# Message-passing layer: both parts of the edge means stacked on 128 partitions, 8 products of 128 rows a step for 12 of 64

## The chip, the core and the metric

The kernel runs on one core of a Trainium2 chip. A core has TensorE (PE, matrix products out of SBUF into PSUM; PEld is its weight load), VectorE (DVE), ScalarE (ACT), GpSimd (POOL), SyncE (SP, which here issues transfers) and 16 DMA engines. They run side by side and wait for one another by semaphores. The metric is the device time of one execution in microseconds, as a median of several runs.

## What is computed

6250 nodes with 256 features, 100,000 edges with 64 features. The edge features are averaged over the edges of each source node, joined with the node's features and a global vector, sent through two dense layers, added to the node's features and normalized:

```python
sums = jax.ops.segment_sum(edge_attr, src, num_segments=n)
counts = jax.ops.segment_sum(jnp.ones((edge_attr.shape[0],), edge_attr.dtype), src, num_segments=n)
edge_attr_agg = sums / jnp.maximum(counts, 1.0)[:, None]
u_expanded = u[batch]
combined = jnp.concatenate([x, edge_attr_agg, u_expanded], axis=1)
h = jax.nn.relu(combined @ W1 + b1)
return h @ W2 + b2
# and around it
x = _layernorm(x + that)
```

W1 has 448 rows (256 for x, 64 for the edge means, 128 for the global vector) and 512 columns, W2 is 512 x 256. All is float32.

## The kernel before

The program has three stages. In the **first** (to about 500 us) the edges are sorted by node in batches, and beside this the part of the hidden layer that depends on x and the global vector is computed into `pre`. In the **second** (about 500 to 735 us) the sorted rows are loaded in pairs of blocks (`sup`, issued by SP, 8 pairs a turn), DVE and ACT make `onehot` masks from them, and PE adds up the sums and counts of all nodes in its PSUM banks (L840). Between the first and the second turn of these loads SP also loads the 64 rows of W1 for the edge means (`w1e_raw`, L453) and W2 (L454). POOL, which has nothing else to do then, cuts both into a high part (as float32r, a shorter format) and a low part, the remainder (L545, L548).

The **third** stage, the layers, is the one that the change is in. DVE makes `means` (125 nodes on the partitions; 50 columns of nodes with 64 features) from the banks in eight instructions (L1166). Then 25 steps follow, each with two columns of 125 nodes, and two sets of buffers b = 0, 1 used in turn. A product in full precision is made of three of shorter ones: high by high, low by high, high by low. Step g consists of:

- `transpose_means` (PE, L864): the 125x64 means of each column, transposed to 64x125, into PSUM (`aggt_p`).
- `save_aggt` (ACT, L655): their high part, to SBUF (`aggt_high`, 64 partitions, 250 columns).
- `low_means` (DVE, L1181): PSUM minus the high part gives the low part (`aggt_low`).
- `first_layer_edges` (PE, L876): for each of 4 blocks of 128 hidden units three products of 64 rows by 250 columns, 12 in all, into `h_p`.
- `hidden_sum` (DVE, L1174): `h_p` added to `pre`, two instructions.
- `relu` (ACT, L661 and L666): `h_high`, the high part, in one instruction, then `pre` itself in two halves.
- `low_hidden` (POOL, L565): `h_low`, two instructions. After it POOL adds b2 to two columns of x (`add_b2`, L556, on `xs`), three steps ahead.
- `second_layer` (PE, L892): 24 products into `y_p`, of which 8 take `h_low`.
- `moments` (DVE, L1189 to L1198): z = y + xs, its statistics, mean and variance. z needs the store of step g-2 from the same buffer to have landed.
- `deviation` (ACT, L670), `finish_norm` (DVE, L1202 reciprocal, L1204 `shift`), `normalize` (ACT, L676), then the store (SP, L469).

Each engine takes its instructions in the order in which they are written, and this order is staggered over the steps. PE: transposes of g+2, L876 of g+1, L892 of g. DVE: moments of g, hidden_sum of g+2, low_means of g+3, finish_norm of g. ACT: deviation of g, save_aggt of g+3, relu of g+2, normalize of g. POOL: low_hidden of g, add_b2 of g+3. DVE and ACT run the first 20 steps as two rounds of a loop over 10 and write the last 5 out.

The lines that the change rewrites most:

```python
for w_part, part in ((0, 0), (1, 0), (0, 1)):
    last = nc.tensor.matmul(h_p[b][:, at:at + NW], w1er[w_part][:, k * P:(k + 1) * P],
                            aggt[b][part][:, :], start=(w_part == part == 0), stop=(part == 1))
```

## Time and profile before

| | |
|---|---|
| median of 3 runs | 879.79 us (876.77 to 879.95) |
| profiled execution | 875.59 us |
| its span in the trace | 873.6 us |
| its granted TensorE clock, mean | 0.972 |
| PE busy | 789.4 us, 90% |
| DVE busy | 702.8 us, 80% |
| ACT busy | 491.8 us, 56% |
| POOL busy | 438.8 us, 50% |
| the layers, from the first instruction on means | 736.70 us to the end |

The profile shows one execution. Its span is 2 us shorter than that execution's own time, and that time is 4.2 us under the median. A row of the timeline is an instruction (or a merged run of them) with its start, its length, its engine and line, and in brackets how long its engine had been idle before it and who ended that. Lengths of neighbours on one engine overlap a little. What an engine does while another holds up the end costs nothing, so shares of busy time are only the beginning.

### The profile page before, as it was taken

The numbers are of one execution on the slowest core, as the hardware profiler recorded it, in microseconds if no ns is written. First come the engines' busy times: TensorE is split into PE (matmuls) and PEld (weight loads), VectorE is DVE, ScalarE is ACT, GpSimd is POOL, SyncE is SP. The second block draws the span as 40 slices with busy tenths as digits, with TensorE's granted clock in tenths as the row PEclk, the third lists the DMA queues.
The fourth block names the chain that finished last, engine by engine and source line by source line (L and its number), as shares of the span: only waits on it lengthen the run. The fifth ranks groups of instructions, "written<-read, shape, count | busy, mean of one in ns | idle before, by whom it ended". The sixth has DMA issues, their size and how long they took to land.

```text
span 873.6 us, 32606 instructions
## 1 busy us (share of the span) xinstructions
PE 789.4 (90%) x11466; PEld 732.5 (84%) x11467; DVE 702.8 (80%) x2328; ACT 491.8 (56%) x998; POOL 438.8 (50%) x429
## 2 busy tenths in 40 slices
PE   5578999999999999999999679898988887999996
PEld 4367888989888999889999579898888886999995
DVE  8599978988888888888996078888889887577785
ACT  1143666556665666556666445555555553678775
POOL 3055667877777777777777220000001000678883
PEclk9778999999999999999999989999999999899998
DMA  8244677677667776677664289999997780011111
GB/s 196 89 135 138 185 165 230 202 222 230 209 205 215 230 231 207 210 221 229 198 191 168 92 292 271 288 278 277 281 277 231 221 250 27 18 55 49 59 59 61
DMA packets 170992, 161.40 MB, mean 185 GB/s; under 512 B 111654, under 2 KB 151705, under 8 KB 170830
## 3 DMA queue, kind: packets, MB, share of 16 engines
q1 hardware_dynamic: 152398, 102.18, 42.5%
q0 software_dynamic: 18560, 58.82, 19.2%
q8 instruction: 16, 0.26, 0.1%
q14 instruction: 18, 0.15, 0.1%
HBM read 95.32 MB, written 65.63 MB: 184 GB/s over the span
## 4 chain that ended last, share of the span: by engine, by line
PE 67%; DVE 9%; DMA 8%; POOL 6%; issue 6%; ACT 2%; SPq 1%; DVEq 0%; ACTq 0%; POOLq 0%
PE ps L840 22%; PE ps L785 20%; PE ps L892 8%; PE ps L717 7%; POOL sorted_rows L530 5%; PE ps L876 5%; DMA sorted_rows<-payload,idx 4%; DVE onehot L1135 2%; DVE perm L1045 2%; POOL sorted_rows L536 2%; DMA attr_buf<-in_edge_attr 1%; DMA where_d<-where 1%; ACT payload L586 1%; PE ps L734 1%; PE ps L772 1%
## 5 line engine op out<-in xcount | busy, mean ns | idle before, releaser
L530 POOL DMA_INDIRECT sorted_rows<-payload,idx x264 | 296.2, 1122 | 141.9 <-issue 56.4
L785 PE MATMUL ps<-attr_buf,perm 128*128 128x198 bf16 x3168 | 312.3, 256 | 16.9 <-DVE perm L1045 13.0
L785 PEld LDWEIGHTS ps<-attr_buf,perm 128*128 128x128 bf16 x3168 | 290.8, 97 | 35.0 <-issue 17.6
L586 ACT CAST payload<-ps 128x792 bf16<-128x792 f32 x264 | 213.3, 828 | 187.7 <-PE ps L785 164.1
L1045 DVE TENSOR_SCALAR perm<-place_of,pos 128x470 bf16<-128x470 int16 x792 | 234.6, 356 | 19.5 <-PE ps L785 18.0
L1135 DVE TENSOR_SCALAR onehot<-node_of,sup 128x256 bf16<-128x256 int16 x903 | 194.4, 286 | 60.1 <-PE ps L840 28.0
L840 PE MATMUL ps<-sup,onehot 128*128 128x65 bf16 x6192 | 202.2, 194 | 32.0 <-DVE onehot L1135 25.2
L840 PEld LDWEIGHTS ps<-sup,onehot 128*128 128x128 bf16 x6192 | 199.7, 98 | 34.7 <-issue 34.7
L642 ACT ACTIVATE apart<-node_of,sup 128x256 bf16<-128x256 int16 x129 | 65.5, 508 | 109.1 <-PE ps L840 104.3
L565 POOL TENSOR_TENSOR h_low<-pre,h_high 128x500 fp32r<-128x500 f32 x50 | 62.2, 1261 | 113.8 <-ACT pre L666 113.8
L717 PE MATMUL ps<-xt,w1x 128*128 128x125 f32 x800 | 100.0, 279 | 4.7 <-ACT xt L591 4.7
L556 POOL TENSOR_TENSOR xs<-xs,b_all 125x256 f32<-125x256 f32 x50 | 35.6, 733 | 134.9 <-DMA xs<-in_x 134.9
L717 PEld LDWEIGHTS ps<-xt,w1x 128*128 128x128 f32 x800 | 94.5, 194 | 6.6 <-ACT xt L591 5.8
L950 DVE TENSOR_TENSOR attr_buf<-attr_buf 128x576 f32<-128x576 f32 x88 | 66.0, 751 | 19.8 <-DMA attr_buf<-in_edge_attr 19.4
L597 ACT ACTIVATE pre<-ps,hid_bias 128x125 f32 (+1 forms) x200 | 56.7, 374 | 21.6 <-PE ps L717 21.6
L957 DVE TENSOR_TENSOR attr_buf<-attr_buf 128x576 f32<-128x576 f32 x88 | 65.4, 744 | 0.0
L645 ACT ACTIVATE onehot<-apart 128x256 bf16<-128x256 bf16 x129 | 53.8, 417 | 4.1
L892 PE MATMUL ps<-w_high,h_high 128*125 128x256 f32 x200 | 52.7, 296 | 0.0
L892 PE MATMUL ps<-w_low,h_high 128*125 128x256 f32 x200 | 50.0, 283 | 0.0
L661 ACT ACTIVATE h_high<-pre 128x1000 fp32r (+1 forms) x25 | 26.0, 1041 | 25.9 <-DVE pre L1174 25.9
L892 PEld LDWEIGHTS ps<-w_high,h_high 128*125 128x125 f32 x200 | 37.5, 188 | 3.3 <-issue 0.2
L963 DVE TENSOR_REDUCE pos<-ps 128x450 f32 (+1 forms) x44 | 27.4, 622 | 14.7 <-PE ps L772 13.8
(144 smaller groups left out, 686.5 us busy)
## 6 DMA issues: line engine op xcount, KB each, us to landing
sup<-sorted_rows SPq DMA_DIRECT2D x129, 396.0 KB, 4.1
attr_buf<-in_edge_attr SPq DMA_DIRECT2D x43, 576.0 KB
xs<-in_x SPq DMA_DIRECT2D x10, 560.0 KB
out<-z SPq DMA_DIRECT2D x25, 224.0 KB
x_stage<-in_x SPq DMA_DIRECT2D x47, 112.0 KB
sorted_rows<-payload,idx POOLq DMA_INDIRECT x264
pre<-jump_d SPq DMA_DIRECT2D x1, 1560.0 KB, 10.6
pre<-first_d SPq DMA_DIRECT2D x1, 780.0 KB, 7.3
```

Of the source, the lines that this page charges most:

```text
L530: pool.indirect_dma_start(out=sorted_rows, out_offset=bass.IndirectOffsetOnAxis(ap=idx[:, n:n + 1], axis=0), in_=payload[s][:, :], in_offs ...
L565: nc.gpsimd.tensor_tensor(h_r[b][1][:, at:end], pre[:, g * KH * NW + at:g * KH * NW + end], h_r[b][0][:, at:end].bitcast(F32), ALU.subtrac ...
L586: nc.scalar.copy(payload[s][:, :].rearrange("p (r w) -> p r w", w=PART), slots_p[s % PSUM_BUFS]).then_inc(s_pay, 1)
L642: nc.scalar.activation(apart[k // 2 % 2][:, :], node_of[:, :], ACT.Abs, scale=-1.0, bias=place_in[k][:, ACT_SLOT, :]).then_inc(s_apart, 1)
L717: last = nc.tensor.matmul(pre_p[:, k * NP:(k + 1) * NP], w1x[:, c, k * P:(k + 1) * P], xt[:, c, :], start=(c == 0), stop=(c == KX - 1))
L785: last = nc.tensor.matmul(slot_p[s % PSUM_BUFS][r].rearrange("p (h f) -> p h f", f=PLANE), places, parts[:, :, s * BT + t, :, 1], start=(t ...
L840: last = nc.tensor.matmul(ps[:, bass.ds(at[k] + h * 512, ROW)], onehot[k % HOT_BUFS][:, r, h * P:(h + 1) * P], sup[k][:, r, part * PLANE:p ...
L892: last = nc.tensor.matmul(y_p[b][0:NP, c * DIM:(c + 1) * DIM], h_r[b][part][:, at:at + NP], w2r[w_part][:, k * DIM:(k + 1) * DIM], start=( ...
L950: nc.vector.tensor_tensor(attr_buf[a][:, 1, at, 0:FEAT], attr_buf[a][:, 0, at, 0:FEAT], high, ALU.subtract).then_inc(s_rest, 1)
L957: nc.vector.tensor_tensor(attr_buf[a][:, 2, at, 0:FEAT], attr_buf[a][:, 1, at, 0:FEAT], middle, ALU.subtract).then_inc(s_low, 1)
L1045: last = nc.vector.tensor_scalar(perm[s][:, t, :], place_of[:, :], pos[:, bass.ds(c * CT + (s * BT + t), 1)], None, ALU.is_equal)
L1135: last = nc.vector.tensor_scalar(onehot[k % HOT_BUFS][:, r, :], node_of[:, :], place_in[k][:, r, :], None, ALU.is_equal)
```

## The change

W1's 64 rows for the means are loaded twice, one above the other, on 128 partitions, and the high part is made of both copies. The low part has its 64 rows above 64 rows of zeros. DVE splits the means before they are transposed: a copy gives the high part, a subtraction the low part, both into `mean_parts`, 64 features beside 64. One transpose of 125x128 then brings the high part on partitions 0 to 63 and the low part on 64 to 127, and ACT saves all 128 with one copy (`aggt`). The first product of a block is W1's doubled high part by both parts (two of the three products before), the second is the low part above zeros by the same (the third). So each step has 8 products of 128 rows for 12 of 64.

`low_means` goes; `split_means` comes, two instructions on DVE, and stands ahead of `moments` in a step. `transpose_means` waits for it. Four of the eight means instructions come before the first two splits, four after.

```diff
-        w1er = [sb(f"w1e_{part}", [FEAT, HID], F32R) for part in ("high", "low")]
-        w1e_raw = sb("w1e_raw", [FEAT, HID])[:, :]
+        w1er = [sb(f"w1e_{part}", [P, HID], F32R) for part in ("high", "low")]
+        w1e_raw = sb("w1e_raw", [P, HID])[:, :]
...
-        aggt = [[sb(f"aggt{b}_{part}", [FEAT, NW], F32R) for part in ("high", "low")] for b in range(2)]
+        mean_parts = [sb(f"mean_parts{b}", [P, 2, 2, FEAT], F32R) for b in range(2)]
+        aggt = [sb(f"aggt{b}", [P, NW], F32R) for b in range(2)]
...
-            sp.dma_start(w1e_raw, w1[DIM:DIM + FEAT, :]).then_inc(s_w2, 16)
+            for half in range(2):
+                sp.dma_start(w1e_raw[half * FEAT:(half + 1) * FEAT, :], w1[DIM:DIM + FEAT, :]).then_inc(s_w2, 16)
...
-            for n, (low, whole, high) in enumerate(((w1er[1], w1e_raw, w1er[0]), (w2r[1], w2_raw, w2r[0]))):
-                pool.wait_ge(s_w_hi, n + 1)
-                nc.gpsimd.tensor_tensor(low[:, :], whole, high[:, :].bitcast(F32), ALU.subtract).then_inc(s_w_lo, 1)
+            nc.gpsimd.memset(w1er[1][:, :].bitcast(F32), 0.0).then_inc(s_w_hi, 1)
+            for n, (low, whole, high) in enumerate(((w1er[1][0:FEAT, :], w1e_raw[0:FEAT, :], w1er[0][0:FEAT, :]),
+                                                    (w2r[1][:, :], w2_raw, w2r[0][:, :]))):
+                pool.wait_ge(s_w_hi, 3)
+                nc.gpsimd.tensor_tensor(low, whole, high.bitcast(F32), ALU.subtract).then_inc(s_w_lo, 1)
...
             def transpose_means(g, b):
-                pe.wait_ge(s_aggt_lo, g + 1)
+                if g >= 2:
+                    pe.wait_ge(s_aggt, g - 1)
+                pe.wait_ge(s_mean_lo, g + 1)
                 for c in range(2):
-                    at = (g * 2 + c) * FEAT
-                    last = nc.tensor.transpose(aggt_p[b][:, c * NP:(c + 1) * NP], means[0:NP, at:at + FEAT],
-                                               ident[0:NP, 0:NP])
+                    both = mean_parts[b][0:NP, c, :, :].rearrange("p s f -> p (s f)")
+                    last = nc.tensor.transpose(aggt_p[b][:, c * NP:(c + 1) * NP], both.bitcast(F32), ident[0:NP, 0:NP])
...
             def first_layer_edges(g, b):
-                pe.wait_ge(s_aggt_lo, g + 3)
+                pe.wait_ge(s_aggt, g + 1)
...
-                    for w_part, part in ((0, 0), (1, 0), (0, 1)):
-                        last = nc.tensor.matmul(h_p[b][:, at:at + NW], w1er[w_part][:, k * P:(k + 1) * P],
-                                                aggt[b][part][:, :], start=(w_part == part == 0), stop=(part == 1))
+                    nc.tensor.matmul(h_p[b][:, at:at + NW], w1er[0][:, k * P:(k + 1) * P], aggt[b][:, :],
+                                     start=True, stop=False)
+                    last = nc.tensor.matmul(h_p[b][:, at:at + NW], w1er[1][:, k * P:(k + 1) * P], aggt[b][:, :],
+                                            start=False, stop=True)
...
-            def low_means(g, b):
-                dve.wait_ge(s_aggt, g + 1)
-                nc.vector.tensor_tensor(aggt[b][1][:, :], aggt_p[b], aggt[b][0][:, :].bitcast(F32),
-                                        ALU.subtract).then_inc(s_aggt_lo, 1)
+            def split_means(g, b):
+                dve.wait_ge(s_aggt_p, g + (PAIR - 1))
+                two = means[0:NP, bass.ds(g * (2 * FEAT), 2 * FEAT)].rearrange("p (c f) -> p c f", f=FEAT)
+                high, low = mean_parts[b][0:NP, :, 0, :], mean_parts[b][0:NP, :, 1, :]
+                nc.vector.tensor_copy(high, two).then_inc(s_mean_hi, 1)
+                dve.wait_ge(s_mean_hi, g + 1)
+                nc.vector.tensor_tensor(low, two, high.bitcast(F32), ALU.subtract).then_inc(s_mean_lo, 1)
...
             def step(m, s, left=STEPS):
                 g = m * PAIR + s
+                if left > 3:
+                    split_means(g + 3, 1 - s % 2)
                 moments(g, s % 2, m * PAIR + s // 2 * 2)
                 if left > 2:
                     hidden_sum(g + 2, s % 2)
-                if left > 3:
-                    low_means(g + 3, 1 - s % 2)
                 finish_norm(g, s % 2)
...
-            low_means(0, 0)
-            low_means(1, 1)
+            for k in (6, 7, 0, 1):
+                mean(k)
+            dve.wait_ge(s_agg, 4)
+            split_means(0, 0)
+            split_means(1, 1)
+            for k in (2, 3, 4, 5):
+                mean(k)
+            split_means(2, 0)
             hidden_sum(0, 0)
             hidden_sum(1, 1)
-            low_means(2, 0)
```

The places on which most depends. First DVE, in the loop over the steps, from the last instruction of hidden_sum on, as it was (line, operation, output and inputs, shape; ISA and REGISTER_ALU rows only compute addresses and waits):

```order
L1174 ISA
L1174 TENSOR_TENSOR pre<-ps,pre 128x2x2x125
L1180 REGISTER_ALU
L1181 TENSOR_TENSOR aggt1_low<-ps,aggt1_high 64x250
L1201 REGISTER_ALU
L1202 RECIPROCAL rstd<-std 125x2
L1204 SCALAR_TENSOR_TENSOR shift<-mv,rstd 125x2
L1185 ISA
L1189 ISA
L1189 TENSOR_TENSOR z<-ps,xs 125x256
```

Here the low part of the means stands between hidden_sum and the reciprocal, and z follows shift. The same place on DVE with the change:

```order
L1184 TENSOR_TENSOR pre<-ps,pre 128x2x2x125
L1214 REGISTER_ALU
L1215 RECIPROCAL rstd<-std 125x2
L1217 SCALAR_TENSOR_TENSOR shift<-mv,rstd 125x2
L1190 REGISTER_ALU
L1193 ISA
L1193 COPY mean_parts0<-means 125x2x64
L1195 TENSOR_TENSOR mean_parts0<-means,mean_parts0 125x2x64
L1198 ISA
L1202 ISA
L1202 TENSOR_TENSOR z<-ps,xs 125x256
```

The instruction behind hidden_sum is gone, and a copy and a subtraction stand between shift and the next z.

Second PE, at the start of the layers, from the end of the second stage on, as it was (`aggt0_high` is the high part of buffer 0):

```order
L850 MATMUL ps<-zeros 128x455 x6
L850 MATMUL ps<-zeros 128x260 x2
L864 MATMUL ps<-ident,means 64x125 x4
L876 MATMUL ps<-aggt0_high,w1e_high 128x250
L876 MATMUL ps<-aggt0_high,w1e_low 128x250
L876 MATMUL ps<-aggt0_low,w1e_high 128x250
```

Four transposes of means are followed by three products for each block. The same place with the change:

```order
L858 MATMUL ps<-zeros 128x455 x6
L858 MATMUL ps<-zeros 128x260 x2
L874 MATMUL ps<-ident,mean_parts0 128x125 x2
L874 MATMUL ps<-ident,mean_parts1 128x125 x2
L884 MATMUL ps<-aggt0,w1e_high 128x250
L886 MATMUL ps<-aggt0,w1e_low 128x250
```

The transposes now give 128 rows, and of each three products two are left.

## Rows read from the trace of the kernel before

**Rows 1.** Busy time by stretch: PE, PEld, DVE, ACT, POOL, clock, DMA share, GB/s.
```profile
690.00:700.00 10.00, 8.42 (x267) 8.30 (x264) 8.02 (x39) 5.05 (x12) 0.00 (x0) 1.00 0.75 216
740.00:750.00 10.00, 8.99 (x40) 8.18 (x41) 4.13 (x9) 3.52 (x6) 2.78 (x3) 0.52 0.00 0
770.00:780.00 10.00, 10.00 (x82) 9.35 (x81) 7.57 (x22) 7.76 (x15) 8.12 (x9) 1.00 0.16 51
```

**Rows 2.** Chain that ended last: start, length, what; a step, then the end.
```profile
795.06 1.59 PE ps L876 x12
796.65 3.02 PE ps L892 x24
799.67 0.22 PE ps L864 x2
...
857.69 0.77 DVE z L1189 x2
...
863.21 0.99 ACT z L676 x2
...
866.63 0.77 DVE z L1189 x2
```

**Rows 3.** Timeline of DVE at the start of the layers: start, length, idle before.
```profile
736.70 3.94 DVE L1166 TENSOR_TENSOR means<-ps,rcount 128x256 f32<-128x256 f32 x8
...
743.97 1.26 DVE L1174 TENSOR_TENSOR pre<-ps,pre 128x500 f32<-128x500 f32 x2 [2.69 <-PE ps L876]
...
751.66 0.75 DVE L1189 TENSOR_TENSOR z<-ps,xs 125x256 f32<-125x256 f32 x2 [2.71 <-PE ps L892]
```

**Rows 4.** Timeline of DVE in the layers, some instructions of several steps.
```profile
775.74 0.75 DVE L1189 TENSOR_TENSOR z<-ps,xs 125x256 f32<-125x256 f32 x2 [0.48 <-PE ps L892]
...
779.37 0.16 DVE L1204 SCALAR_TENSOR_TENSOR shift<-mv,rstd 125x2 f32<-125x2 f32 x1
...
784.31 0.61 DVE L1204 SCALAR_TENSOR_TENSOR shift<-mv,rstd 125x2 f32<-125x2 f32 x1
785.40 0.75 DVE L1189 TENSOR_TENSOR z<-ps,xs 125x256 f32<-125x256 f32 x2 [0.47 <-PE ps L892]
...
808.45 0.46 DVE L1204 SCALAR_TENSOR_TENSOR shift<-mv,rstd 125x2 f32<-125x2 f32 x1
```

**Rows 5.** Timeline of ACT: normalize, of the step whose z began at 775.74.
```profile
781.36 1.08 ACT L676 ACTIVATE z<-z,shift,rstd 125x256 f32<-125x256 f32 x2
```

**Rows 6.** Timeline of POOL in the layers.
```profile
781.01 2.49 POOL L565 TENSOR_TENSOR h_low<-pre,h_high 128x500 fp32r<-128x500 f32 x2 [0.84 <-ACT pre L666]
783.47 1.43 POOL L556 TENSOR_TENSOR xs<-xs,b_all 125x256 f32<-125x256 f32 x2
...
808.15 1.43 POOL L556 TENSOR_TENSOR xs<-xs,b_all 125x256 f32<-125x256 f32 x2
```

**Rows 7.** z alone (ns min/median/max) and shift in the groups (busy, mean ns).
```profile
L1189 DVE TENSOR_TENSOR z<-ps,xs x50: 411/419/426, 751.7 to 867.0; 125x256 f32<-125x256 f32 x50
...
L1204 DVE SCALAR_TENSOR_TENSOR shift<-mv,rstd 125x2 f32<-125x2 f32 x25 | 9.4, 377 | 0.9
```

**Rows 8.** The page, costliest groups: onehot's (busy us, mean ns, idle before).
```profile
L1135 DVE TENSOR_SCALAR onehot<-node_of,sup 128x256 bf16<-128x256 int16 x903 | 194.4, 286 | 60.1 <-PE ps L840 28.0
```

**Rows 9.** Timeline in the second stage: SP's queue, POOL and DVE.
```profile
504.60 0.63 SPq L453 DMA_DIRECT2D w1e_raw<-in_L_gnn_W  x1
...
517.31 2.34 POOL L548 TENSOR_TENSOR w_low<-z,w_high 128x1024 fp32r<-128x1024 f32 x1
...
517.39 2.35 DVE L1135 TENSOR_SCALAR onehot<-node_of,sup 128x256 bf16<-128x256 int16 x1 [2.81 <-PE ps L840]
```

**Rows 10.** Timeline of PE: second and last product of one step's L876.
```profile
800.04 0.27 PE L876 MATMUL ps<-aggt_high,w1e_low 64*128 64x250 f32 x1
...
801.20 0.28 PE L876 MATMUL ps<-aggt_low,w1e_high 64*128 64x250 f32 x1
```

**Rows 11.** Timeline of PE's weight loads: a pair of transposes of x.
```profile
307.79 0.23 PEld L708 LDWEIGHTS ps<-ident,x_stage 125*128 125x128 f32 x2
```

More of the change, by code:

```diff
@@ L267, in build @@
         y_p = [bank(4 + b) for b in range(2)]
-        aggt_p = [bank(6 + b, NW)[0:FEAT, :] for b in range(2)]
+        aggt_p = [bank(6 + b, NW) for b in range(2)]
         s_fill = sem("s_fill")
@@ L327, in build @@
         s_aggt = sem("s_aggt")
-        s_aggt_lo = sem("s_aggt_lo")
+        s_mean_hi = sem("s_mean_hi")
+        s_mean_lo = sem("s_mean_lo")
         s_h_p = sem("s_h_p")
@@ L654, in save_aggt @@
                 act.wait_ge(s_h_p, g + 1)
-                nc.scalar.copy(aggt[b][0][:, :], aggt_p[b]).then_inc(s_aggt, 1)
+                nc.scalar.copy(aggt[b][:, :], aggt_p[b]).then_inc(s_aggt, 1)
             def relu(g, b):
@@ L1144, in _ @@
             dve.sem_inc(s_z, 4)
-            dve.sem_inc(s_aggt_lo, 2)
             for b in range(2):
@@ L1163, in _, with mean @@
             mean_of = means[:, :].rearrange("p (b h f) -> p h b f", h=2, f=FEAT)
-            for k in (6, 7, 0, 1, 2, 3, 4, 5):
+            def mean(k):
                 lo, hi, sums = table_bank(k)
```

2 lines of the change are left out of this document (1 added, 1 removed).

## The prediction

> **What bounds the kernel now.** By the table above, TensorE (PE) is busy for 90% of the span at a granted clock of 0.972. The change touches only the last stage, the two layers over 25 steps, so next I read the busy time by stretch [rows 1]: there PE is busy all the time at clock 1.00, with VectorE (DVE) at 7.57 of 10 us, ScalarE (ACT) at 7.76 and GpSimd (POOL) at 8.12. All are loaded; PE is merely first. The chain of waits [rows 2] says the same: one step is 0.22 us of transposes, 1.59 us for the 12 products of L876 and 3.02 us for the 24 of L892, 4.83 us in all, and nothing else. It runs so from the first z at 751.66 us [rows 3] to that of step 22 at 857.69 us [rows 2]; this is 106.03 us for 22 steps.
>
> Then I followed the other engines through a step [rows 4 to 6], because a PE that gets faster is worth only what they leave. Write z(g) for the start of z in step g. It is 775.74 in one step and 785.40 two steps on, so 9.66 us for two; DVE is idle for 0.48 and 0.47 us before these. From z(g) a chain runs on: hidden_sum, ACT's h_high and pre, then POOL's two h_low instructions at 781.01, 5.27 us after z(g), then at once POOL's two xs additions from 783.47 us, ending at 784.90 us, 9.16 us after z(g). That last event is half a microsecond ahead of z(g+2). It matters if something on DVE has to wait for it.
>
> **Something does.** The shift instruction (L1204) works on 125x2 numbers, yet its mean is 377 ns [rows 7]. Asked for at 779.37 us it takes 0.16 us; asked for at 784.31 it lasts to 784.92 [rows 4], and POOL's second addition ends at 784.90. Asked at 808.45 it ends at 808.91, where the first of the two additions from 808.15 (1.43 us for both) ends, so it can slip in between two POOL instructions. Both inputs of shift are in SBUF. z has one of its two in PSUM, and its 50 instructions take 411 to 426 ns, whatever POOL is doing. An instruction with one tensor as its input shows the same in the stage before: a onehot, 286 ns on average on the page [rows 8], takes 2.35 us at 517.39 and ends just behind POOL's w_low (517.31, 2.34 us) [rows 9]. So some DVE instructions with all operands in SBUF stand still for as long as a POOL instruction runs. Today only shift does so in the layers, inside DVE's idle time.
>
> The Trainium skill, SBUF — State Buffer, section Who interferes with whom, gives this as a rule: a DVE instruction in a two-port mode (copies and scalar operations between SBUF tiles can be), or with two SBUF inputs while GpSimd reads SBUF, blocks fully against a GpSimd instruction. The rows above agree. It speaks against this change, because the old low_means read PSUM and one SBUF tile, and both instructions of the new split have only SBUF operands. Without it the sum would be that of the first rival.
>
> **Part 1, PE.** Eight products for twelve. Inside L876 ten starts take 1.16 us (800.04 to 801.20 [rows 10]), 0.116 us a product; these have 64 rows and 250 columns. Those of L892 have 128 rows and 256 columns and come at 3.02/24 = 0.126 us with their gaps, so 128 rows cost no more than 64 beyond the extra columns. Four fewer are -0.46 us a step. The transposes grow from 64 to 128 columns of means; their nearest row, the transposes of x (125x128, L708), has 0.23 us for the weight loads of a pair [rows 11], against 0.22 us for a pair here [rows 2], so I take 0. PE could then run a step in 4.37 us.
>
> **Part 2, DVE.** low_means (0.40 us) goes; split_means comes, ahead of moments: a copy of 125x128, a wait for it, a subtraction of 125x128. In the rows, 125x2 takes 0.16 us and 125x256 takes 419 ns [rows 4, 7], so 125x128 is half way, 0.29 us; the copy lies between the same ends, and I take 0.25 us. With a wait between and one on each side (I take 0.18 us for the three, more than the idle 0.01 to 0.1 us between instructions that follow without one) the pair is 0.72 us; bounds 0.42 (two at 0.16 and 0.1) to 1.14 (two at 0.419 and 0.3). Queued behind it are moments, hidden_sum and everything down to the output; and PE's transposes of that step, which used to be long free to go, now wait for its end.
>
> Where does it fit? DVE arrives at shift when POOL is at its additions. Then shift, copy and subtraction must come behind them: shift ends 9.18 us after z(g) (784.92), and 0.72 us more put z(g+2) 9.90 us after z(g) instead of 9.66. If the copy slips in between the two additions, POOL is put back by as much, which gives the same. The same holds for odd and even steps, since each POOL round starts from its own z. So **the step is 4.95 us, bound by DVE behind POOL, and PE idles 0.5 us of it**: +0.24 us for each of 11 pairs, +2.6 us. With the bounds of the split the pair of steps is 9.60 to 10.32 us, so -0.7 to +7.3 us. If only the subtraction waits and the copy runs beside POOL, the pair is shorter by the copy and its wait, about 9.6 us, -0.7 us in all: this counts as the same case.
>
> **Part 3, ACT.** save_aggt copies 128 rows instead of 64 in the same columns: as many columns as before, so as long, and ACT is busy for 7.76 of 10 us [rows 1]. Nothing.
>
> **Part 4, the start of the layers.** Before, the means (3.94 us) come first, then the two low parts and the first products, and hidden_sum at 743.97 us [rows 3]. Now four of the eight means instructions (about 1.9 us) and two splits (0.72 each, POOL idle here) come first; products start near 740.3 us, at a clock of about 0.52 [rows 1], the lower of its two levels (1.2 GHz, not 2.4), 8 at twice 0.116 us, 1.9 us, so h_p is ready at 742.2. DVE meanwhile does the other four means and a third split, to 742.8 us. hidden_sum is 1.2 us earlier. PE's next turn of L876 has four slow products less too, but L892 then waits a little for h_high and h_low. I take z(0) **1.5 us** earlier (0.8 to 2.2).
>
> **Part 5, the stage before.** SP issues a second load of the W1 rows between two turns of sup loads (0.63 us [rows 9]), 128 KB more through the DMA engines (216 GB/s at three quarters busy [rows 1]: 0.6 us at that rate, less if they have room); POOL's work on the weights, which blocks DVE, gets a memset of 128x512 (at most half of w_low's 2.34 us, which is on 128x1024). Bounds 0.2 to 1.8 us; **+0.8 us** taken: the loads are a turn ahead, which covers a part, but DVE's time is spent.
>
> **Part 6, the end.** From z(22) to the end, 15.9 us, nothing is removed: z(24) waits for the store of step 22 in the same buffer [rows 2].
>
> Sum: +2.6 - 1.5 + 0.8 = +1.9 us. The profiled execution took 875.59 us (span 873.6); 877.5 us for it, and on the median of 879.79 us, which lies 4.2 us above, 881.7 us.
>
> **Rivals.** (a) **DVE does not wait for POOL**: the split runs earlier in the step, in the time that shift stands still now. For it: the evidence is small operands and another stage; no row has this subtraction. Even then PE's 4.37 us isn't reached: from z(775.74) to the end of normalize (781.36 + 1.08) are 6.70 us, and in the tail normalize's end at 864.20 to z at 866.63 is 2.43 us, through the store that frees the buffer. That makes 9.13 us for two steps: 11 x -0.53 = -5.8, with the rest -6.5 us, 873.3 us. (b) **PE's saving is paid whole**: 24 steps x -0.46 = -11.0, with +0.8: 869.6 us. This needs the store to land 0.4 us sooner; nothing speaks for it. (c) **Slower**: the subtraction is asked for after POOL's next h_low has begun, and stands behind 1.25 us (half of 2.49 [rows 6]). The additions end 9.16 us after the z of two steps ago, h_low begins 5.27 us after the last z. After a short step of 4.58 us (PE's 4.37 and 0.2 to z) the additions end at 4.58, and the subtraction is asked for at about 4.98, 0.29 us ahead of h_low. It decides once the waits and the copy are 0.3 us longer than I take them. Price 1.25 us each; in 4 of 11 pairs 5.0 us: 886.7 us; in all, 14 us. (d) **The clock falls** in PE's new gaps: in the stage before PE was 84% busy at clock 1.00 [rows 1], so hardly; its price would be tens of microseconds.
>
> **How the numbers follow.** Half a per cent, 4.4 us, is about what a measurement here can tell from no change. The forecast has 0.56 (of that 0.04 beyond +4.4 us through its upper bound), (a) 0.20, (b) 0.04, (c) 0.18, (d) 0.02. Faster 0.24, same 0.52, slower 0.24. The forecast's own range is 877 (-0.7 - 2.2 + 0.2) to 888 us (+7.3 - 0.8 + 1.8); for 8 in 10 the range takes in (a) and a good part of (c): 873.0 to 888.0 us.
>
> **What would show it.** Right: in the layers the copy and the subtraction of the split with means well above 0.29 us, ending with POOL's instructions; z idle before it not for PE but for nothing; PE idle 0.4 to 0.6 us a step ahead of its transposes, waiting for the split; the products for L876 down to 1.12 us a step; POOL's sum of busy time unchanged. (a) shows as split instructions at 0.25 to 0.29 us and z waiting for the DMA of its store. (c) shows as single instructions of 1 us and more. If the transposes or the products of 128 rows come at more than 0.13 us, part 1 is wrong; if the first z isn't 0.8 to 2.2 us earlier after its own stage start, part 4 is.

## The result: 0.55% faster

| | before | after |
|---|---|---|
| median of 20 runs each, side by side | 879.44 us (876.32 to 881.32) | 874.17 us (871.67 to 876.47) |
| ratio of the times | | 0.9945, 95% interval 0.9933 to 0.9957 |
| profiled execution, its span | 875.59 us, 873.6 us | 875.22 us, 873.3 us |

The forecast was 881.7 us, no change. The time fell by 5.3 us; it lies in the range (873.0 to 888.0 us), but on the side that had a chance of 0.24.

The two profiled executions differ by 0.4 us only, the medians by 5.3. So the spans can't be subtracted; they have to be cut into stages. The table does this for all executions profiled in this study: stage 1 ends at the first product with zeros that opens stage 2; stage 2 ends at the first `rcount`; then come the time to z(0), the loop from z(0) to z(22), and the rest. Each column is a difference of two starts in the timelines. The experiments are explained in the next section.

| execution | stage 1 | stage 2 | rcount to z(0) | z(0) to z(22) | z(22) to end |
|---|---|---|---|---|---|
| before, first profile | 498.3 | 237.2 | 16.2 | 106.0 | 15.9 |
| before, again | 501.6 | 236.7 | 17.0 | 106.7 | 16.0 |
| after, first profile | 500.5 | 238.2 | 14.1 | 105.0 | 15.5 |
| after, again | 498.4 | 237.8 | 13.8 | 104.1 | 15.5 |
| after, five buffers for z | 502.0 | 239.2 | 14.1 | 104.2 | 15.2 |
| after, without POOL's additions | 500.9 | 238.1 | 14.1 | 101.7 | 15.5 |
| after, without additions, five buffers | 502.6 | 237.9 | 13.9 | 99.0 | 15.2 |
| after, one addition of 512 columns | 503.9 | 238.1 | 13.9 | 105.8 | 15.5 |
| after, eight additions of 64 | 499.0 | 237.5 | 13.7 | 109.9 | 15.4 |
| after, 12 products | 562.1 | 238.3 | 14.9 | 106.7 | 15.5 |
| split from PSUM | 565.5 | 239.4 | 14.7 | 103.3 | 15.9 |
| split from PSUM, five buffers | 558.6 | 237.4 | 14.7 | 99.9 | 15.2 |
| split from PSUM, five buffers, on another chip | 502.1 | 237.8 | 16.1 | 99.7 | 15.2 |
| before, with the change's weights | 562.8 | 239.2 | 16.9 | 106.0 | 15.5 |

Stage 1, which no edit touches, wanders by up to 5.6 us (498.3 to 503.9) and hides the change in single spans; on one chip it took 60 us more for every kernel, with the later stages as elsewhere. The stages after it repeat within 1 us: two executions of one kernel differ by up to 0.5 us in stage 2, 0.8 in the start and 0.9 in the loop. With two executions each of before and after, the means give +1.06 us in stage 2, -2.63 to z(0), -1.84 in the loop and -0.48 at the end: -3.9 us of the 5.3. That is just inside the interval of the ratio (3.8 to 5.9 us). Where the other 1.4 us are isn't shown; two executions a side can't tell.

### The profile after

Busy time by stretch; the columns are those of [rows 1], and the second and third row answer to its second and third.

```profile
core 0: us, PE busy (x) PEld busy (x) DVE busy (x) ACT busy (x) POOL busy (x), PEclk, DMA share, GB/s
740.00:750.00 10.00, 7.01 (x30) 5.79 (x30) 8.47 (x19) 3.45 (x7) 0.98 (x1) 0.66 0.00 0
770.00:780.00 10.00, 8.39 (x69) 7.89 (x68) 9.34 (x27) 7.36 (x15) 8.01 (x9) 1.00 0.19 61
```

PE, full before (10.00), is busy for 8.39 of 10 us; DVE has gone from 7.57 to 9.34. The clock stays at 1.00. VectorE is now first, as the forecast said. Three rows of the waits in the layers (engine and line, whom it waited for, us in total, times, longest), from 752 to 858 us:

```profile
PE ps L874 <- DVE mean_parts L1195: 12.2, 20, 1.2
ACT std L678 <- DVE mv L1211: 6.0, 8, 1.6
DVE z L1202 <- DMA out<-z: 3.5, 4, 1.2
```

PE's transposes (L874) wait for the split's subtraction in 20 steps, 0.61 us each; the prediction had 0.4 to 0.6. The new split, the shift and z one by one (ns min/median/max, first and last start); for z and shift this answers to [rows 7]:

```profile
L1193 DVE CAST mean_parts<-means x25: 213/216/1125, 741.9 to 852.4; 125x128 fp32r x20, 125x128 fp32r<-125x128 f32 x5
L1195 DVE TENSOR_TENSOR mean_parts<-means,mean_parts x25: 291/702/1249, 742.2 to 852.6; 125x128 fp32r<-125x128 f32 x25
...
L1217 DVE SCALAR_TENSOR_TENSOR shift<-mv,rstd x25: 160/400/759, 756.2 to 869.3; 125x2 f32<-125x2 f32 x25
...
L1202 DVE TENSOR_TENSOR z<-ps,xs x50: 406/415/426, 752.8 to 867.1; 125x256 f32<-125x256 f32 x50
```

Undisturbed, the subtraction takes 0.29 us; its median is 0.70. z, with one input in PSUM, stays at 0.42. So the standing still behind POOL is there. But it costs less than I took, and three steps of the timeline show why, DVE's first and POOL's below:

```profile
806.00 0.76 DVE L1202 TENSOR_TENSOR z<-ps,xs 125x256 f32<-125x256 f32 x2 [0.20 <-PE ps L902]
...
809.30 0.63 DVE L1217 SCALAR_TENSOR_TENSOR shift<-mv,rstd 125x2 f32<-125x2 f32 x1
809.86 0.21 DVE L1193 CAST mean_parts<-means 125x128 fp32r x1
810.11 0.70 DVE L1195 TENSOR_TENSOR mean_parts<-means,mean_parts 125x128 fp32r<-125x128 f32 x1
810.73 0.74 DVE L1202 TENSOR_TENSOR z<-ps,xs 125x256 f32<-125x256 f32 x2
...
814.03 0.47 DVE L1217 SCALAR_TENSOR_TENSOR shift<-mv,rstd 125x2 f32<-125x2 f32 x1
814.42 0.85 DVE L1193 CAST mean_parts<-means 125x128 fp32r x1
815.30 0.29 DVE L1195 TENSOR_TENSOR mean_parts<-means,mean_parts 125x128 fp32r<-125x128 f32 x1
815.62 0.76 DVE L1202 TENSOR_TENSOR z<-ps,xs 125x256 f32<-125x256 f32 x2
...
833.38 0.66 DVE L1217 SCALAR_TENSOR_TENSOR shift<-mv,rstd 125x2 f32<-125x2 f32 x1
...
834.54 0.76 DVE L1202 TENSOR_TENSOR z<-ps,xs 125x256 f32<-125x256 f32 x2
```

```profile
809.18 1.48 POOL L564 TENSOR_TENSOR xs<-xs,b_all 125x256 f32<-125x256 f32 x2
811.28 2.50 POOL L573 TENSOR_TENSOR h_low<-pre,h_high 128x500 fp32r<-128x500 f32 x2 [0.62 <-ACT pre L674]
813.74 1.45 POOL L564 TENSOR_TENSOR xs<-xs,b_all 125x256 f32<-125x256 f32 x2
...
832.61 1.42 POOL L564 TENSOR_TENSOR xs<-xs,b_all 125x256 f32<-125x256 f32 x2
```

In the first step the shift waits for the first of POOL's two additions (809.18, half of 1.48 us, so to 809.92), the cast goes in between the two, and the subtraction waits out the second (to 810.66). z starts 0.07 us after POOL is done. In the second the shift is asked for at 814.03, behind h_low, and waits for the first addition (813.74, half of 1.45 us, so to 814.47); the cast waits for the second, to 815.19, and only the 0.29 us subtraction comes after it: z starts 0.43 us after POOL. The third has the order of the prediction: the shift waits to the end of both additions (834.03), cast and subtraction come behind, and z starts 0.51 us after POOL. The additions themselves are put back little: where the cast goes in between, they take 1.47 to 1.51 us for 1.43 [rows 6].

### The profile page after: what moved, and what is told of

It is laid out like the page before. It is cut to its first block, busy times and chain, and to the rows that moved or that the text cites. A ratio compares the mean times of both kernels' runs of the same rounds, so it can differ in the third digit from the quotient of the medians.

```text
span 873.3 us, 32490 instructions
## 1 busy us (share of the span) xinstructions
PE 772.6 (88%) x11366; PEld 717.2 (82%) x11367; DVE 721.2 (83%) x2353; ACT 491.7 (56%) x998; POOL 439.4 (50%) x430
## 4 chain that ended last, share of the span: by engine, by line
PE 53%; DVE 13%; DMA 10%; issue 8%; POOL 8%; ACT 4%; SPq 1%; DVEq 1%; ACTq 0%; PEldq 0%; POOLq 0%
PE ps L848 22%; PE ps L793 18%; PE ps L725 6%; POOL sorted_rows L536 6%; DMA sorted_rows<-payload,idx 5%; DVE onehot L1145 3%; POOL sorted_rows L542 2%; DVE perm L1055 2%; PE ps L902 2%; DMA out<-z 2%; DVE pre L1184 1%; DVE stats L1207 1%; DMA where_d<-where 1%; ACT payload L594 1%; PE ps L742 1%
## 5 line engine op out<-in xcount | busy, mean ns | idle before, releaser
L1055 DVE TENSOR_SCALAR perm<-place_of,pos 128x470 bf16<-128x470 int16 x792 | 239.2, 362 | 19.5 <-PE ps L793 17.5
L960 DVE TENSOR_TENSOR attr_buf<-attr_buf 128x576 f32<-128x576 f32 x88 | 66.0, 751 | 15.3 <-DMA attr_buf<-in_edge_attr 14.9
L902 PE MATMUL ps<-w_high,h_high 128*125 128x256 f32 x200 | 50.1, 283 | 0.3 <-issue 0.3
L973 DVE TENSOR_REDUCE pos<-ps 128x450 f32 (+1 forms) x44 | 27.4, 623 | 15.2 <-PE ps L780 12.5
L902 PEld LDWEIGHTS ps<-w_low,h_high 128*125 128x125 f32 x200 | 37.4, 187 | 0.0
```

Source lines behind the costliest of these rows:

```text
L902: last = nc.tensor.matmul(y_p[b][0:NP, c * DIM:(c + 1) * DIM], h_r[b][part][:, at:at + NP], w2r[w_part][:, k * DIM:(k + 1) * DIM], start=( ...
L960: nc.vector.tensor_tensor(attr_buf[a][:, 1, at, 0:FEAT], attr_buf[a][:, 0, at, 0:FEAT], high, ALU.subtract).then_inc(s_rest, 1)
L1055: last = nc.vector.tensor_scalar(perm[s][:, t, :], place_of[:, :], pos[:, bass.ds(c * CT + (s * BT + t), 1)], None, ALU.is_equal)
```

## The experiments

Theory L: DVE stands still behind POOL's additions ("POOL's lock" from here on), and this takes most of PE's saving. Rivals: the store of z limits the loop; PE's saving was never to be had; the gain of the loop is chance. All runs were made beside the kernel before on the same chip.

### Both kernels again

> The kernel before once more, to split its time by stage. The two profiled executions differ by 0.3 us in span, the medians by 5.3 us, and in the trace the changed kernel's first stage (no edit there) took 2.2 us longer. Theory 1, chance: the first stage wanders by some us from one execution to the next, and the layers of before always take the same, since PE paces them: z(0) to z(22) 106.0 us (105.7 to 106.3), means to z(0) 15.0 us. Theory 2: the change makes the first stage slower: then the first stage of this run ends at 498 us again.

> The changed kernel once more, same questions. Theory 1: the first stage ends anywhere between 496 and 501 us; z(0) to z(22) lies between 102.5 and 106 us, by how many stores land late in it (in the first trace 105.0 us with four landings of over 3.5 us after the end of normalize). Theory 2: the first stage ends at 500.5 us again. Ratio to before 0.9945.

Before: 880.09 us in its one execution (879.75 us the median of all of before on that chip). After: 875.82 us, ratio 0.995 (0.9927 to 0.9972). The gain repeats, and by the table it lies in the same stages. Stage 1 ended at 501.6 us in before and at 498.4 in after, the other way round than in the first pair, so nothing shows that the change makes it longer. Two expectations for before were missed: the loop took 106.7 us (105.7 to 106.3 expected; in one pair of its steps z waited 1.76 us for a store), and means to z(0) took 15.8 us (15.0). So before, too, varies: by 0.6 us in the loop and 0.8 us in the start. In this execution of after no z waited for a store until the tail, and yet the loop was only 0.9 us shorter than in the first: the store isn't what limits it.

### Five buffers for z

```diff
-        s_store = [sem(f"s_store{b}") for b in range(2)]
+        z_more = sb("z_more", [P, 2 * 2 * DIM])
+        z = z + [z_more[:, b * 2 * DIM:(b + 1) * 2 * DIM] for b in range(2)] + [w1e_raw]
+        s_store = [sem(f"s_store{b}") for b in range(5)]
```

> The changed kernel with five buffers for z instead of two, so no z waits for the store of two steps before. Theory A, the store of z holds up some steps (late packets): z(0) to z(22) falls from 105.0 to 102 to 103 us (pairs of steps at 9.3 us, which the split behind POOL sets), time 2 to 4 us under the changed kernel's 874.2. Theory B, the stores only fill idle time that DVE's wait for POOL leaves: no change, 873 to 875.5 us. The end of the kernel is shorter in both, since the last z doesn't wait either (about 1.3 us).

872.73 us, ratio 0.992 (0.9891 to 0.995). Its loop, 104.2 us, lies between the two executions of after, with no wait for a store left; the end is 0.3 us shorter, not the expected 1.3. The rival "store" is out for the change as it stands. (The ratio is lower than that of after, but the intervals overlap, and the stages show 0.3 us at the end and nothing in the loop.)

### Without POOL's additions

```diff
                 if g + B2_AHEAD < STEPS:
-                    add_b2(g + B2_AHEAD)
+                    pool.sem_inc(s_xb, 2)
```

> The changed kernel without POOL's additions of b2 from step 3 on (b2 is missing from the output of those steps). POOL is then busy for 2.5 us a step instead of 4.0, and done before DVE gets to the split. Theory L, DVE's instructions between SBUF tiles stand still while POOL runs: the subtraction's median falls from 702 ns to 0.29 us, and the pairs of steps to the store's 9.0 to 9.2 us: z(0) to z(22) 100 to 102 us, 3 to 5 us under the changed kernel. Rival, the subtraction is slow by itself or waits for something else: its median stays at 0.7 us, and the time at 873 to 875 us.

871.76 us, ratio 0.9926 (0.9899 to 0.9953), and the loop falls from 104.1 or 105.0 to 101.7 us. The groups of DVE show how far the standing still went (line, busy us, mean ns, idle before; 769 to 849 us), and the waits what came next:

```profile
L1195 DVE TENSOR_TENSOR mean_parts<-means,mean_parts 125x128 fp32r<-125x128 f32 x17 | 5.0, 293 | 0.6
L1193 DVE CAST mean_parts<-means 125x128 fp32r (+1 forms) x17 | 3.9, 227 | 1.1 <-issue 0.5
L1217 DVE SCALAR_TENSOR_TENSOR shift<-mv,rstd 125x2 f32<-125x2 f32 x18 | 3.4, 189 | 0.6
```

```profile
DVE z L1202 <- DMA out<-z: 8.7, 14, 1.6
PEld ps L902 <- POOL h_low L573: 4.7, 16, 0.3
```

The three means add up to 709 ns. In the first profile of the change they are 528, 416 and 439 (772 to 852 us), together 1383: 0.67 us of standing still a step. Of it only (104.5 - 101.7) / 22 = 0.13 us a step is gained, because the store takes over. This run also takes 1.5 us of work a step from POOL; that the standing still counts and not POOL's work is shown by the split from PSUM below, which keeps the additions. Most pairs of steps here last 9.14 to 9.26 us; rival (a) of the prediction had 9.13 for a loop bound by the store.

### Without the additions and with five buffers

The two edits above together.

> The change without GpSimd's additions of b2 from the fourth step on (the output lacks b2 there) and with five buffers for z: both the wait behind GpSimd and the wait for the store are gone. Theory 'store next, then one chain of two steps through all four engines': pairs of 8.9 to 9.1 us as in the kernel with the split from PSUM and five buffers (9.07), 98.5 to 100.5 us in the loop, against 101.7 with two buffers. Rival 'the store wait only showed what the chain took anyway': loop within 0.5 us of 101.7.

869.1 us, ratio 0.9851 (0.9802 to 0.9899), from 4 runs. The loop is 99.0 us, pairs of 8.9 to 9.1 in most places: the first theory holds. Behind POOL's lock comes the store, and behind that a third limit, which the last experiment shows. So theory L is right about the wait and too strong about its price. Of the 10.1 us that the prediction's 0.46 us a step come to, the loop gains 1.8 in the change, 4.7 without the lock and 7.4 without the lock and the wait for the store: 2.8 us hung on the lock alone.

### One addition for two, eight for two

```diff
-                for c in range(2 * g, 2 * g + 2):
-                    column_x = xs[0:NP, c * DIM:(c + 1) * DIM]
-                    nc.gpsimd.tensor_tensor(column_x, column_x, b2_all[0:NP, :], ALU.add).then_inc(s_xb, 1)
+                two = xs[0:NP, 2 * g * DIM:(2 * g + 2) * DIM].rearrange("p (c n) -> p c n", n=DIM)
+                nc.gpsimd.tensor_tensor(two, two, b2_all[0:NP, :].unsqueeze(1).to_broadcast([NP, 2, DIM]),
+                                        ALU.add).then_inc(s_xb, 2)
```

> The change with GpSimd's two additions of b2 of a step (125x256 each, 0.75 us) made by one instruction of 125x512, about 1.45 us, from the fourth step on; same result, same bytes. Theory 'VectorE slips in at the boundary of two of GpSimd's instructions': the boundary is gone, so whatever of cast, subtraction and shift comes while the addition runs waits up to 1.5 us instead of 0.75. In the profile of the change the three have means of 393, 526 and 440 ns in the loop against 213, 291 and 160 free, 0.70 us of waits a step; here I expect 0.9 to 1.3 us a step, longest above 1.2 us for all three, and 105.5 to 108.5 us in the loop (change 104.1 to 105.0). Rival 'GpSimd holds VectorE off for the whole of its burst, boundary or not': no difference, waits at 0.70 and the loop within 0.5 us of the change.

876.16 us, ratio 0.9942 (0.9915 to 0.997), loop 105.8 us, in which one late store cost 1.2 us. The sum of the three means is 1390 ns, so 0.68 us of standing still a step, not 0.9 to 1.3: a miss. The rival's number came, but not its reason. One addition is shorter than two (1.30 us for 1.42 to 1.51), and the waiting falls on the shift or on the cast, here on the cast, DVE first, POOL below:

```profile
812.87 0.16 DVE L1222 SCALAR_TENSOR_TENSOR shift<-mv,rstd 125x2 f32<-125x2 f32 x1
813.07 1.24 DVE L1198 CAST mean_parts<-means 125x128 fp32r x1
814.34 0.29 DVE L1200 TENSOR_TENSOR mean_parts<-means,mean_parts 125x128 fp32r<-125x128 f32 x1
```

```profile
812.93 1.30 POOL L568 TENSOR_TENSOR xs<-xs,b_all 125x512 f32<-125x512 f32 x1
```

The subtraction never waits (291 to 294 ns over all 25), where with two additions it had waits up to 0.4 us in the loop. So nothing slips in any more: at least the subtraction always comes behind POOL's end, and z starts 0.40 us or more after it, never 0.07. Twelve of the first seventeen pairs of steps take 9.59 to 9.65 us and none less than 9.56, where the change has many of 9.2 to 9.3. That the loop is hardly longer (104.6 us without the late store) is because POOL ends earlier: 9.0 us after z for 9.2.

```diff
+                    for q in range(8 * g, 8 * g + 8):
+                        at = q % 4 * 64
+                        part_x = xs[0:NP, q * 64:(q + 1) * 64]
+                        nc.gpsimd.tensor_tensor(part_x, part_x, b2_all[0:NP, at:at + 64], ALU.add).then_inc(s_q, 1)
+                    pool.wait_ge(s_q, (g - 2) * 8)
+                    pool.sem_inc(s_xb, 2)
```

> The change with GpSimd's two additions of a step cut into eight of 64 columns each, from the fourth step on; same result. Theory 'boundary': VectorE waits for at most one short addition (about 0.2 us each plus what eight instructions cost in place of two), so the waits of cast, subtraction and shift fall from 0.70 to 0.2 to 0.45 us a step and the loop to 102 to 104 us, near that of the run without additions (101.7), with more waits for the store. Rival 'burst': waits as in the change or longer, loop 104 to 106 us. If GpSimd's fixed cost an instruction is high, its additions take over 2.2 us a step and h_low comes late; then the loop is no shorter in spite of short waits.

880.04 us, ratio 0.9998 (0.9973 to 1.0024), loop 109.9 us. The standing still falls to 0.33 us a step (237, 297 and 508 ns), as the theory "boundary" had it and "burst" had not. But an addition of 64 columns takes 0.33 us, eight in a row 2.40 us a step for 1.43 to 1.51, so the loop missed the expected 102 to 104 us, and POOL is the bound, as the last sentence of the expectation allowed (waits from 774.5 to 854.5 us):

```profile
PEld ps L911 <- POOL h_low L582: 15.2, 16, 1.2
PE ps L911 <- POOL h_low L582: 11.9, 16, 1.0
DVE z L1211 <- PE ps L911: 11.7, 16, 0.8
```

### Twelve products again

```diff
-                    last = nc.tensor.matmul(h_p[b][:, at:at + NW], w1er[1][:, k * P:(k + 1) * P], aggt[b][:, :],
-                                            start=False, stop=True)
+                    for again in range(2):
+                        last = nc.tensor.matmul(h_p[b][:, at:at + NW], w1er[1][:, k * P:(k + 1) * P], aggt[b][:, :],
+                                                start=False, stop=(again == 1))
```

> The change with twelve products a step instead of eight: the product with W1's low part is done twice, so that its share is added twice to the result. Split, transposes and order of the change stand. It takes back TensorE's saving alone (4 products of 250 columns, about 0.45 us a step). Theory 'TensorE's saving, less what VectorE waits': TensorE's work of a step is back at that of before while the split still waits behind GpSimd: loop 105.5 to 108.5 us, 1.5 to 4 us over the change, start of the layers still 2 us early (about 14 us). Rival 'the loop of the change is bound by the split and GpSimd alone': loop within 0.7 us of the change's 104 to 105 us.

936.2 us, ratio 0.9987 (0.9953 to 1.002), so the gain is gone within the interval. Loop 106.7 us: PE's four products are worth 2.2 us of the loop (one execution against the mean of two, which are 0.9 us apart), of 22 x 0.46 = 10.1 us by the prediction's price. The start is 14.9 us, where about 14 was expected; against the 14.1 us of the first profile of after, with as long at the lower clock level, the products are worth 0.8 us there as well.

### The change's weights alone

```diff
-        w1er = [sb(f"w1e_{part}", [FEAT, HID], F32R) for part in ("high", "low")]
+        w1er = [sb(f"w1e_{part}", [P, HID], F32R) for part in ("high", "low")]
...
-                        last = nc.tensor.matmul(h_p[b][:, at:at + NW], w1er[w_part][:, k * P:(k + 1) * P],
+                        last = nc.tensor.matmul(h_p[b][:, at:at + NW], w1er[w_part][0:FEAT, k * P:(k + 1) * P],
```

(and the double load and the memset of the change)

> The kernel of before with the change's weight preparation alone: W1's last 64 rows loaded twice, high and low part on 128 partitions, GpSimd's memset of the low part, all in stage 2; the layers and their 12 products of 64 rows as before. The step of the prediction (+0.8 us in stage 2, nothing elsewhere): stage 2 longer by 0.5 to 1.5 us (the change showed +1.1), loop 105 to 107 us as before, total +0.5 to +1.5 us over the kernel before. Rival: the +1.1 us of stage 2 is chance between executions, and the time is that of before within 0.3 us.

936.76 us, ratio 0.998 (0.9945 to 1.0015): the total can't tell +1 us from nothing on this chip, and I have no profile of before there. Start (16.9) and loop (106.0) are those of before, so these don't come from the weights. That stage 2 is longer rests on the table: 236.7 and 237.2 us without the double load, 237.4 to 239.4 in twelve executions with it. Its end, 15.5 us, is as short as that of the change, though its layers are those of before.

### The split read from PSUM

Before's order and its `low_means`, but its result goes to partitions 64 to 127 of one tile, ScalarE's copy to 0 to 63, and the 8 products are those of the change.

```diff
-                nc.scalar.copy(aggt[b][0][:, :], aggt_p[b]).then_inc(s_aggt, 1)
+                nc.scalar.copy(aggt[b][0:FEAT, :], aggt_p[b]).then_inc(s_aggt, 1)
...
-                nc.vector.tensor_tensor(aggt[b][1][:, :], aggt_p[b], aggt[b][0][:, :].bitcast(F32),
+                nc.vector.tensor_tensor(aggt[b][FEAT:P, :], aggt_p[b], aggt[b][0:FEAT, :].bitcast(F32),
```

> The kernel of before with the change's 8 products of 128 rows, but the split left where it was: the transposes stay 64 columns wide, ScalarE's copy writes the high part to partitions 0 to 63 of the pair of parts, and VectorE's subtraction, with one operand in PSUM, writes the low part to partitions 64 to 127. So VectorE has no instruction left that touches SBUF alone on large tiles and is put behind GpSimd's additions, and the order of before (means of blocks 6, 7, 0 to 5, no earlier split) stands at the start of the layers. Theory 'the wait behind GpSimd eats the saving': the loop is then as short as the store allows, pairs of steps 9.1 to 9.3 us as in the run without GpSimd's additions (101.7 us from the first to the last step of the loop there), so 101 to 102.5 us in the loop, stage 2 at +1.1 us, start of the layers as before (16.2 to 17, so 2 us later than the change): 873 to 875 us, about equal to the change. Theory 'the saving of TensorE is not to be had in the loop, whatever VectorE does': loop 104 to 106 us and 876 to 879 us.

932.96 us, ratio 0.9941 (0.9909 to 0.9972), as much as the change. The subtraction never stands still now:

```profile
L1184 DVE TENSOR_TENSOR aggt<-ps,aggt x25: 402/412/414, 810.0 to 922.1; 64x250 fp32r<-64x250 f32 x25
```

Fourteen of its first seventeen pairs of steps take 9.15 to 9.28 us, as without the additions. POOL's additions are all there, and the pairs are still as short as without them: it was the split's standing still that cost, and not POOL's work. The loop came to 103.3 and not 102.5 us; one z in it waited 2.65 us for a store. The start was a surprise: 14.7 us, not 16.2 to 17, although this kernel has before's order there.

### The same with five buffers

> The same kernel with five buffers for z instead of two, so that no z waits for the store of the step two before. Theory 'split behind GpSimd first, store second, TensorE third': both of the first two are gone, each step is TensorE's own work less four products, 4.40 to 4.55 us, so pairs of 8.8 to 9.1 us and 97 to 100 us from the first to the last z of the loop; about 869 to 872 us, faster than the change by 2 to 5 us. If VectorE's own work or ScalarE's chain takes over at once, pairs stay at 9.2 or more and the time within 1 us of the run with two buffers.

930.59 us, ratio 0.9913 (0.9877 to 0.9949). On the chip with the short stage 1:

> The kernel with the split from PSUM, 8 products and five buffers for z once more, since on the chip of the last call the first stage took 60 us more than before and scattered. By its stages (loop 99.9 us, 14.7 from the first rcount to z, tail 15.2, stage 2 +1.1) it should be 16.5 us less than the kernel before in the layers' 138.5 us less 1.1, no: 138.1 less 129.8 is 8.3 us, less 1.1 in stage 2, so 7.2 us faster: ratio 0.990 to 0.993. Rival: the gain in the layers is not seen in the total, ratio above 0.995.

872.16 us, ratio 0.9893 (0.9855 to 0.9931), from 6 runs, a little below the expected 0.990 to 0.993; loops 99.9 and 99.7 us. It leaves nothing out and is the fastest such version of this study; its loop is 4.2 to 5.2 us shorter than that of the change. Of its two ratios one has its interval just below that of the change (up to 0.9931 against 0.9933 and more), the other's overlaps it, and its start of the layers (14.7 and 16.1) varies by more than 1 us. So that it beats the change is shown for the loop, and likely for the total.

The chain of waits in the first of its two executions shows the third limit (start, length, what):

```profile
830.66 0.08 DVE pre L1179
830.75 0.51 issue
831.26 0.68 DVE pre L1179
...
832.15 1.05 ACT h_high L666
...
833.30 0.63 ACT pre L671
833.94 0.07 issue
834.00 1.26 POOL h_low L570
835.27 0.04 issue
835.31 2.18 PE ps L897 x16
...
837.69 0.08 DVE z L1194
...
838.48 0.76 DVE stats L1199 x2
...
839.62 0.08 DVE pre L1179
```

No engine is full there (PE, the fullest, 9.45 of 10 us from 822 to 832). A step's hidden_sum, h_high, pre, h_low, second layer, z and statistics run one after the other through all four engines, and the next but one hidden_sum is behind them on DVE: 839.62 - 830.66 = 8.96 us for two steps, where PE alone would need 8.74 by the prediction's 4.37 us a step.

## Why the prediction was right and wrong, step by step

**What bounds, and the wait behind POOL: right.** PE was the bound; the split's instructions stand still behind POOL; VectorE takes PE's place. The rule of the Trainium skill, SBUF — State Buffer, section Who interferes with whom, on which this leant, agrees with every run: the subtraction with two SBUF inputs waits for POOL, the one with an input in PSUM doesn't (0.70 against 0.41 us, medians of the two).

**Part 2, the loop, is the step that failed.** I put 0.72 us behind the end of shift, at POOL's end, 9.18 us after z, and so 9.90 us for a pair: +2.6 us. POOL's end is where I had it: in the step above it is 815.19 - 806.00 = 9.19 us after z. What comes behind it isn't 0.72 us, and this term of the sum is what was wrong. In 30 of the 33 full z of the two profiles of after, between 772 and 852 us and 769 and 849 us, z starts 0.07 to 0.68 us after POOL's last addition; of the other three, two had waited for a store and one followed such a wait. There are two patterns: where the subtraction has stood still (16 times) z comes 0.07 to 0.26 us after POOL, but once; where it hasn't (14 times), 0.40 to 0.68. So pairs of 9.27 us and of 9.6 to 9.7 us are the commonest; the mean of the 11 pairs is 9.54 and 9.46 us. An instruction that stands still ends just behind POOL's: the shift 0.02 us, the cast 0.09 and the subtraction 0.15 us, while free they take 0.16, 0.21 and 0.29. The shift's in [rows 4] had shown this. So of three instructions in a row one or two are absorbed in the standing still, and the cast can slip in between two of POOL's. The order that I had summed, shift to POOL's end and both others behind it, came in 5 of the 30; even there cast and subtraction were through 0.48 us after POOL. I had written: "If the copy slips in between the two additions, POOL is put back by as much, which gives the same." POOL was put back by 0.04 to 0.08 us. The neighbouring sentence, "about 9.6 us, -0.7 us in all", was the better forecast, and it should have been the value and not a remark. A loop of +2.6 us measured -1.8.

**Part 1, PE: right.** The timeline of after has the products of the first layer 0.12 us apart, as before with half as many rows, and the clock stayed at 1.00. The saving is real, and most of it is idle time now: the 12.2 us of waits above.

**Part 3, ACT: right.** `save_aggt` takes 0.348 us with 128 rows and took 0.346 us with 64 (medians).

**Part 4, the start: right in direction, undersized** (-1.5, bounds to -2.2; measured -2.6). The order went as worked out: products from 743.67, hidden_sum at 745.77, 7.0 us after rcount, where before it began 8.5 after it. What I left out is the clock. The rows of after and below them those of before, same stretches (here the last columns are clock, DMA share, GB/s):

```profile
742.00:746.00 4.00, 3.48 (x15) 2.72 (x15) 3.65 (x11) 0.73 (x2) 0.00 (x0) 0.52 0.00 0
746.00:749.00 3.00, 2.72 (x13) 2.46 (x12) 1.97 (x4) 1.71 (x3) 0.00 (x0) 0.50 0.00 0
749.00:752.00 3.00, 2.49 (x21) 2.28 (x20) 2.62 (x3) 2.86 (x6) 2.98 (x3) 1.00 0.00 0
```

```profile
742.00:746.00 4.00, 4.00 (x19) 3.41 (x18) 1.26 (x2) 0.63 (x1) 0.00 (x0) 0.50 0.00 0
746.00:749.00 3.00, 3.00 (x15) 2.78 (x14) 1.58 (x3) 2.00 (x5) 1.78 (x2) 0.50 0.00 0
749.00:752.00 3.00, 3.00 (x23) 2.81 (x23) 0.34 (x1) 2.87 (x4) 3.00 (x4) 0.90 0.03 5
```

PE has nothing to do while DVE makes the means, and falls to the lower level. Microsecond by microsecond, the kernels with before's layers stay on it for 10.2 to 13.7 us (three executions), those with 8 products for 3.4 or 6.8 us (ten executions); one of these (the split from PSUM with five buffers, second time) fell once more for 3.4 us, and it is the one whose z(0) came at 16.1. So a part of the 2.6 us is a clock that returns sooner. How much it is worth, two kernels show: before's layers need 16.2 us to z(0) with 10.2 us at the low level and 16.9 and 17.0 with 13.7; the change and its variants with 8 products need 13.7 to 13.9 us with 3.4 at that level and 14.1 with 6.8. Why it returns sooner wasn't isolated. At the same 6.8 us the run with 12 products needs 14.9 us and the split from PSUM, in before's order, 14.7: so some 0.8 us of the start are the products and 0.7 the order with the earlier split.

**Part 5, the weights: right**, +1.1 us for +0.8 by the two and two executions of before and after. SP's two loads take 1.29 us for 0.63 and the memset 0.52:

```profile
506.77 1.29 SPq L459 DMA_DIRECT2D w1e_raw<-in_L_gnn_W  x2
...
518.76 0.52 POOL L552 MEMSET w1e_low<- 128x512 f32 x1
```

**Part 6, the end**: 0, measured -0.5, and not shown to come from the change, as before's layers with the change's weights end in 15.5 us too. From z(22) to ACT's last normalize the two chains are alike (857.79 to 869.45, and 857.69 to 869.33, so 11.66 and 11.64 us); the difference lies behind that, in the last store and the end of the program, not in the work.

**The rivals.** (a) needed that DVE not wait, and it does; the median is nearly (a)'s 873.3 us, but for other reasons: its loop of -5.8 us was -1.8, and start and end gave more than I took. Its price for a loop bound by the store, 9.13 us a pair, was what the run without additions showed. (b) needed pairs of 8.74 us; even without the additions and with five buffers they took 9.0 on average. (c), a subtraction behind h_low, happened once in after, at 750.40 us before the first z, where z still waited 1.19 us for PE after it; in the loop the subtraction was always through before h_low began, because less lay behind POOL than I had put there. (d) no.

Put into the sum, the measured terms are -1.84 - 2.63 + 1.06 - 0.48 = -3.9 us, 875.9 us on the median of the prediction. The sign turned on one term of 2.6 us that was 4.4 us off, beside one that was 1.1 us too small. That the range took in the result is owed to its width and to rival (a), which it was drawn to include and which did not happen.

## What to carry to other kernels

When an instruction must stand still for another engine's, don't add its own time to the other's end: here what waited ended within 0.15 us of it, and a short one slipped in between two instructions of the other engine, so only what comes after the last one counts. Before a split is moved ahead of a transpose, look where its operands lie: reading one of them from PSUM kept VectorE out of GpSimd's way at the same number of products. And where the other engines are three quarters full, little of a saving on the full one may be paid (here about a fifth, 2.2 us of 10.1), until the next limits, here the lock, then the buffer of the store, then the chain through all four, are opened in their turn.

## What the runs showed that was not expected

- GpSimd's additions of 125 partitions take 0.33 us for 64 columns, 0.75 for 256 and 1.30 for 512, so about 2.2 ns a column and 0.19 us an instruction. Cutting its work finer to let VectorE in cost more than the lock did (loop 109.9 us for 104.5).
- The time on the lower clock level at the start of the layers is not fixed: 10.2 to 13.7 us before, 3.4 or 6.8 at first with 8 products. A difference of 3.4 us moves z(0) by 0.2 us in the change and by 0.7 to 0.8 in before; in the split from PSUM with five buffers the second fall goes with 1.3 us.
- Some stores land late, with nothing in the kernel's rows that explains it. In after, the one that freed the buffer for 792.06 took 3.32 us from the queue (1.95 us for one in the tail); in that stretch the DMA view has a packet of another queue, that for instructions, which the stretch with a store in time (783 to 787 us) does not have. In the loops of all runs z waited eight times for over 0.9 us for a store, and six times such a packet had started 2.7 to 3.6 us before z; but the loops with five buffers and other stores have such packets too. Whether it is the cause wasn't tried.
